# Group norm and masked batch norm on one core: a ring of eight tiles in place of ten

## What is computed

```python
def _gn(v, G=32, eps=1e-5):              # per image, over groups of 2 channels
    g = v.reshape(B_, G, C_ // G, H_, W_)
    return ((g - mean(g)) / sqrt(var(g) + eps)).reshape(v.shape)

def _L0_conv_ref(x):                     # masked batch norm, mean not subtracted
    m = x.sum(axis=1) != 0               # places whose channel sum is not zero
    ... mean and var per channel over the masked places of all images ...
    out = jnp.where(m[:, None, :, :], x * inv[None, :, None, None], x)
    return out

x = x + _L0_conv_ref(_gn(x))
```

## Time and profile before

| what | value |
|---|---|
| median of 3 runs | 1295.04 us (1294.75 to 1295.29) |
| the profiled execution: own time / span | 1294.88 us / 1293.2 us |
| moved by DMA | 537.58 MB, mean 416 GB/s |
| DMA busy, share of 16 engines | q1 52.3%, q10 49.0% |
| busy: ACT, DVE, PE, POOL | 816.4 (63%), 796.5 (62%), 741.7 (57%), 535.1 us (41%) |
| load of a tile, issue to landing (median) | 17.7 us |
| store of a tile, issue to landing (median) | 29.9 us |
| TensorE's mean granted clock | 0.775 |

### The profile page before, as it was taken

How to read it: one execution, slowest core, us unless ns; L and a number is a source line. 1 busy time by engine, 2 the same in 40 slices (tenths; PEclk the granted TensorE clock), 3 DMA queues, 4 the chain that set the end, 5 groups by cost and what they waited for, 6 DMA issues and landing times.

```text
span 1293.2 us, 10692 instructions
## 1 busy us (share of the span) xinstructions
PE 741.7 (57%) x2882; PEld 302.4 (23%) x2882; DVE 796.5 (62%) x1892; ACT 816.4 (63%) x950; POOL 535.1 (41%) x504
## 2 busy tenths in 40 slices
PE   0766654566545665456654566544665446654475
PEld 0222222222222222122221222212222122222232
DVE  6776666566665666655666556665566655666563
ACT  0777555775557755567655676556765567755575
POOL 0055333454334544345443444434443444533450
PEclk9988767887678876688766887667887678866788
DMA  9999999999999999999999999999999999999997
GB/s 378 415 421 420 421 421 421 422 420 420 421 421 421 420 421 421 421 421 420 421 421 421 421 421 420 421 420 421 421 421 421 420 420 421 418 421 418 420 414 281
DMA packets 135469, 537.58 MB, mean 416 GB/s; under 512 B 4336, under 2 KB 4336, under 8 KB 135408
## 3 DMA queue, kind: packets, MB, share of 16 engines
q1 hardware_dynamic: 69936, 276.83, 52.3%
q10 hardware_dynamic: 65472, 260.05, 49.0%
HBM read 268.44 MB, written 268.44 MB: 415 GB/s over the span
## 4 chain that ended last, share of the span: by engine, by line
DMA 60%; ACT 15%; PE 11%; DVE 7%; issue 5%; SPq 0%; ACTq 0%
DMA out_dram<-slots 37%; DMA slots<-in_x_dram 23%; ACT slots L346 11%; PE flush L421 6%; ACT fresh L343 4%; DVE stats L471 2%; DVE spread L454 2%; PE stay L417 1%; PE stay L418 1%; PE small_ps L386 1%; PE small_ps L396 1%; DVE dev L517 1%; PE small_ps L397 1%; ACT sums L343 0%; SPq L237 0%
## 5 line engine op out<-in xcount | busy, mean ns | idle before, releaser
L471 DVE BATCH_NORM_STATS2 stats<-slots 128x6 f32<-128x512 f32 x1024 | 631.5, 680 | 437.8 <-DMA slots<-in_x_dram 436.5
L346 ACT ACTIVATE slots<-slots,out_bias,out_scale 128x1024 f32<-128x1024 f32 x512 | 622.4, 1245 | 2.3 <-DVE out_bias L528 1.3
L325 POOL TENSOR_TENSOR sums<-fresh,sums 128x512 f32<-128x512 f32 x360 | 458.8, 1274 | 363.6 <-ACT fresh L343 363.6
L421 PE MATMUL flush<-slots,weights 128*64 128x512 f32 x1536 | 442.0, 695 | 42.2 <-ACT fresh L343 40.6
L343 ACT ACTIVATE fresh<-flush,group_bias 128x512 f32<-128x512 f32 x360 | 246.5, 685 | 51.8 <-PE flush L421 51.8
L302 POOL TENSOR_TENSOR weights<-pair_sum,group_rstd 128x256 f32<-128x256 f32 (+1 forms) x128 | 73.2, 602 | 357.5 <-DVE group_bias L508 357.5
L421 PEld LDWEIGHTS flush<-slots,weights 128*64 128x64 f32 x1536 | 131.7, 156 | 295.9 <-issue 294.3
L358 ACT ACTIVATE by_image<-by_image,eps 128x16 f32<-128x16 f32 x32 | 9.8, 307 | 242.2 <-DVE by_image L495 241.8
L417 PE MATMUL stay<-slots,weights 128*64 128x512 f32 x512 | 140.0, 606 | 0.0
L418 PE MATMUL stay<-minus_mean,weights 128*64 128x512 f32 x512 | 138.1, 593 | 0.0
L386 PE MATMUL small_ps<-spread,group_avg 128*128 128x64 f32 x64 | 21.8, 443 | 183.3 <-DVE spread L491 183.3
(11 more groups left out here) (52 smaller groups left out, 234.5 us busy)
## 6 DMA issues: line engine op xcount, KB each, us to landing
slots<-in_x_dram SPq DMA_DIRECT2D x127, 2048.0 KB, 17.7
out_dram<-slots ACTq DMA_DIRECT2D x124, 2048.0 KB, 29.9
out_dram<-slots SPq DMA_DIRECT2D x16, 512.0 KB, 5.1
slots<-in_x_dram SPq DMA_DIRECT2D x4, 512.0 KB, 13.6
```

Of the source, the lines that this page charges most:

```text
L325: pool.tensor_tensor(into, fresh[:, n % FRESH_BUFS, :], into, ALU.add).then_inc(added, 1)
L346: nc.scalar.activation(out_in_ring(u, i), image_in_ring(u, i), ACT.Identity, bias=out_bias[:, u % 2, i:i + 1], scale=out_scale[:, u % 2, i ...
L421: nc.tensor.matmul(into, weight, source, start=True, stop=True).then_inc(image_summed, 1)
L471: last = V.bn_stats(stats[:, u % 2, k * BLOCK_STATS:(k + 1) * BLOCK_STATS], source)
```

## The change

The ring has eight slots, and slots 8 and 9 of `slots` stay outside it, so the tensor is as large as before. Slot 8 holds the unit matrix at the start and the last unit's images 0 to 3 at the end; slot 9 holds `not_zero`. Three waits fall away: SP's for the matrices, ACT's for the store of tile 118, DVE's for the store of tile 119. Load j now waits for the store of tile j - 8. No instruction is added, and none changes its place on its engine.

```diff
--- before.py
+++ after.py
@@ -17,7 +17,8 @@
 BLK = 512
 HALVES = 2
 TILE_IMAGES = 4
-RING = 10
+RING = 8
+PLACES = 10
 FRESH_BUFS = 3
 FLUSH_BANKS = 3
 KEPT_BANKS = 4
@@ -42,7 +43,7 @@
     BLOCK_STATS = 2 * TRIPLE
     FOLDS = 2 * BLOCKS
     FOLD_N = BLK // 2
-    assert UNIT_C == 2 and BLOCKS == 2 and ROWS * BLOCKS == P and RING * TILE_N == 10 * 4096
+    assert UNIT_C == 2 and BLOCKS == 2 and ROWS * BLOCKS == P and PLACES * TILE_N == 10 * 4096
 
 
 
@@ -83,7 +84,7 @@
         def sem(name):
             return ctx.enter_context(nc.semaphore(name))
 
-        slots = sb("slots", [P, RING * TILE_N])
+        slots = sb("slots", [P, PLACES * TILE_N])
         weights = sb("weights", [P, 2, B, ROWS])
         fresh = sb("fresh", [P, FRESH_BUFS, BLK])
         sums = sb("sums", [P, ADDS, BLK])
@@ -114,7 +115,7 @@
         pair_sum = sb("pair_sum", [P, ROWS])
         minus_mean = sb("minus_mean", [P, 2, B])
         minus_pair_sum = sb("minus_pair_sum", [P, ROWS])
-        unit_matrix = slots[:, (RING - 1) * TILE_N:(RING - 1) * TILE_N + P]
+        unit_matrix = slots[:, RING * TILE_N:RING * TILE_N + P]
 
         n_part = sb("n_part", [P, B])
         n_row = sb("n_row", [P, 1])[:, :]
@@ -126,8 +127,8 @@
         mask = held[:, 0:HALF // 2].bitcast(U8).rearrange("p (a n) -> p a n", a=HALVES)
 
 
-        APART_TILE, NOT_ZERO_TILE = TILES - RING, TILES - RING + 1
-        not_zero = slots[:, NOT_ZERO_TILE % RING * TILE_N:NOT_ZERO_TILE % RING * TILE_N + B * BLK // 4].bitcast(U8).rearrange(
+        APART_PLACE, NOT_ZERO = RING, RING + 1
+        not_zero = slots[:, NOT_ZERO * TILE_N:NOT_ZERO * TILE_N + B * BLK // 4].bitcast(U8).rearrange(
             "p (k n) -> p k n", k=B)
         first_g = held[:, 6144:6144 + UNITS * B]
         first_work = held[:, 6656:6656 + UNITS * B]
@@ -181,9 +182,11 @@
         MASK_MOVES = UNIT_C * BLOCKS
         GENERAL_TILES = UNITS * HALVES
 
+        def in_place(k):
+            return slots[:, k * TILE_N:(k + 1) * TILE_N].rearrange("p (i n) -> p i n", i=TILE_IMAGES)
+
         def in_ring(j):
-            at = j % RING * TILE_N
-            return slots[:, at:at + TILE_N].rearrange("p (i n) -> p i n", i=TILE_IMAGES)
+            return in_place(j % RING)
 
         def in_dram(rows, j):
             i = j % UNIT_TILES * TILE_IMAGES
@@ -196,7 +199,7 @@
             return stats[:, u % 2, :].rearrange("p (i f t) -> p i f t", i=B, t=TRIPLE)
 
         def out_in_ring(u, i):
-            return in_ring(APART_TILE)[:, i, :] if u == LAST and i < APART else image_in_ring(u, i)
+            return in_place(APART_PLACE)[:, i, :] if u == LAST and i < APART else image_in_ring(u, i)
 
         def wait_for_sum(engine, u, i):
 
@@ -228,9 +231,6 @@
         def _(sp):
 
             for j in range(TILES):
-                if j == RING - 1:
-
-                    sp.wait_ge(matrices_ready, MATRICES)
                 if j >= RING:
                     sp.wait_ge(stored[j % RING], 16 * (j // RING))
                 if j < TILES - 1:
@@ -360,8 +360,6 @@
                 nc.scalar.activation(bn_std, bn_var_ps, ACT.Sqrt, bias=eps[:, 1:2]).then_inc(sqrt_out, 1)
                 act.wait_ge(scale_ready, (u + 1) * 2)
                 for i in range(B):
-                    if u == LAST and i == 0:
-                        act.wait_ge(stored[APART_TILE % RING], 16 * (APART_TILE // RING + 1))
                     if u < LAST or i >= APART:
                         wait_for_sum(act, u, i)
                     if u < LAST and i in flushed:
@@ -554,7 +552,6 @@
                                            in1=sums[:, flushed.index(i), :], op0=ALU.subtract, op1=ALU.not_equal,
                                            accum_out=n_part[:, i:i + 1]).then_inc(compared, 1)
 
-            dve.wait_ge(stored[NOT_ZERO_TILE % RING], 16 * (NOT_ZERO_TILE // RING + 1))
             for i in sum_order(LAST):
                 count(i)
             dve.wait_ge(counted, len(kept))
```

## The result

| | before | after |
|---|---|---|
| median | 1295.03 us (1294.75 to 1295.29) | 1355.24 us (1354.36 to 1357.28, 4 runs) |
| the profiled execution: own time / span | 1294.88 / 1293.2 us | 1354.87 / 1353.1 us |
| ratio | | 1.0467, 95% interval 1.0449 to 1.0485 |

I had forecast 1315 with a range up to 1348. The way was right, the size was not.

The account below looks back on a forecast made before the run. Data movement was taken as the bound, 16.78 MB per unit at 421 GB/s. Start +14, steady part +14 and end -8 summed to 20 us over the profiled 1294.88, so 1315 us, range 1301 to 1348.

Parts of the forecast that it names:

- Bound and loop: Data movement bounds the kernel; with eight slots the loop closes in one unit through its first store: 16.6 + S + L.
- Steps (1) to (3): The dropped waits of SP for the matrices, ACT for store 118 and DVE for store 119: each worth nothing.
- Step (4): The ring: load j waits for store j-8, giving a one-unit loop of 40.0 us; cadence taken as 40.7.
- replay: Stepping both DMA queues through one unit in step (4): load 13.3 us, next first store due at 40.0.
- Step (5): The start: load 8 waits for store 0 and load 12 lands at 108.9 instead of 94.89, costing 14 us.
- Step (6): The steady part: 28 units at 0.5 us more each, costing 14 us.
- Step (7): The end, from tile 124's landing: 65 us where it was 73.4, giving back 8 us.
- rival A: The loop stays at the engines' pace, cadence 40.17; only start and end count: 1301 us; chance 0.14.
- Rival B: Latency bounds the loop outright; shared transfers take about 1 us more, cadence 42.0: 1352 us; sign 400 GB/s or less; chance 0.28.
- middle case: The forecast case itself: 1306 to 1327 us, cadence 40.3 to 41.1; chance 0.48.
- Rival C: Not slower: shallower queues run faster, eight tiles moving at 426 GB/s, cadence 39.7: 1287 us; chance 0.10.

Follow-up runs that it names:

- run with the chain free: The changed kernel, but DVE takes no block of unit u+1 inside unit u's chain, so it doesn't wait for tile 4u+4: 1300.35 us, ratio 1.0044.
- run with the ring alone: The kernel before with a ring of eight, but without the freed places and with the three waits kept: 1353.99 us, ratio 1.0458.

## Why the prediction was wrong, step by step

- **Bound and loop.** Right: the loop closes in one unit, through the first store, with 16.6 (measured 16.7) of compute in it. The run with the chain free shows the link itself.
- **Steps (1) to (3).** Right, by the run with the ring alone.
- **Step (4), the loop of 40.0, "just on the 40.17 that the engines need".** This failed. The replay let each transfer begin 1.4 after an issue of 0.4, also beside a running one. Measured, from the start of the issue and so against 1.8, it is 4.4 or 2.1 for the store and 3.5 for the load. Against the 10.0 that the replay has for the store counted from the start of its issue, it took 11.0 in the mean; against 13.3 the load took 14.3: 2.0 in all, and 40.0 became 42.0. As the loop lay at the knee, where its length and the engines' pace are the same, nearly all of it counted. I had the load of 13.9 beside stores in my rows, 0.6 over the replay, and the first store's 14.3 over its 12.9, and added only the load's. The trace of before showed the late beginning itself, had I looked at its packets: the first packet of that store came 3.7 after its issue, that of that load 3.5.
- **Step (5), 14 at the start.** Measured 16.1, again by the two transfers: store 4 took 13.9 for my 12.4, load 12 took 14.3 for 13.3. **Step (6), 14 = 28 x 0.5.** Measured 28 x 1.81 = 50.5; that is 36.5 of the miss of 40. **Step (7), -8.** Measured -6.6.
- Start and end together I had at +6, with the cadence unchanged, as rival A, 1301. The run with eight tiles and a free chain is that case: 1300.35.
- **Rival B**, 1352 with a cadence of 42.0, is what happened (1355, 41.98). Its sign, 400 GB/s or less, came too (400 between 110 and 1200). I gave it 0.28 and cut the range at a cadence of 41.9 (by my own sum that is 1349, not 1348, and the 40.3 of the middle case is 1305, not 1306; neither slip matters). With the loop just at the knee and every known error of the replay on one side, the latency-bound case was the likelier one, and a range up to 44.8 for both transfers shared would have held it.
- The Trainium skill's fixed cost of about 2.0 us per DMA ("DMA: Bandwidth & Descriptors", two cost components) stands there for transfers that GpSimd issues, and I used it for those of SP and ACT. By it the loop would have been under the engines' pace and the time 1301. The trace disagrees where it matters: alone, overhead is 2.7 for the load and 1.6 for the store (7.7 and 6.6 less 5.0), around that figure, but a transfer that begins beside another has 1 to 4 us more ahead of its first packet. In these runs it was near one figure only for a DMA that is alone.
- **Rival C** has no ground: fewer tiles in flight never moved over 422 GB/s.

## What to carry to other kernels

Before a ring is shortened, write down which load waits for which store, and through which chain: a ring of a whole number of units can close the loop over one unit where one tile more closes it over two, and that was worth 57 us here, ten to nine tiles only 3. Where a replay of such a loop comes out just at the pace of the bound, each error of its parts counts in full and on the slow side alone, so forecast the case behind the knee. Price a transfer by one that begins beside another, and look at GB/s, for in the 5 us windows above DMA's busy share stays at 1 while it loses a quarter of its rate.

## What the chip showed that I had not expected

A tile's transfer of 2.097 MB that is issued 1 to 3 us after one on the other queue has its first packet after 4.0 to 5.1 us, against 0.9 to 1.1 alone; 4.4 us after it, 2.1 to 2.4. In that time a single load runs at 264 GB/s (364 alone, its start included). Splitting either side, or both, into four transfers does not help. With three tiles in the running queue it is the same (4.3 to 5.0), three running loads make 343 to 348 GB/s meanwhile (417 alone), and each transfer that joins so costs 0.5 to 0.8 us in all. Where both queues always held a tile (the kernel before, nine tiles, the free chain), none began late.
